# A Mamba-style layer on eight cores: the prefix's convolution and state moved into the main input projection

## The reference, cut to what matters

```python
x = L0_attn_u                                  # [2, 8192, 2048]
xn = _layernorm(x, axis=-1)
# s = recurrent branch
zxbcdt = u @ W_in.T                            # 2048 -> 10304
z, xBC, dt = jnp.split(zxbcdt, [D_INNER, D_INNER + CONV_DIM], axis=-1)
conv = conv_b
for k in range(D_CONV):                        # 4 taps along the sequence
    conv = conv + xp[:, k:k + l, :] * conv_w[:, k]
xBC = jax.nn.silu(conv)
x, B, C = jnp.split(xBC, [D_XB, 2 * D_XB], axis=-1)
dt = jax.nn.softplus(dt + dt_bias);  A = -jnp.exp(A_log)
y = _chunked_scan(xh, dt, A, Bh, Ch, D)        # state carried over the sequence
y = y * jax.nn.silu(z)                         # then a group norm and W_out
g = _silu(_L0_ffn_ref(xn, ...))                # Hadamard transforms, up, gate, down
x = x + s * g
```

## Time and profile before

| what | value |
|---|---|
| median of 2 runs | 10579.05 us (10514.8 and 10643.31) |
| the profiled execution | 10557.54 us |
| its span, slowest core | 10555.9 us |
| spans of the 8 cores | 10456.2 to 10555.9 us |
| granted TensorE clock, mean | 0.755 to 0.761 of full |

### The profile page before, as it was taken

The page is one execution under the profiler, slowest core; times in us unless marked ns, Lnnn a source line. Parts: engine busy times, 40 slices in busy tenths (PEclk is TensorE's granted clock), DMA queues, the critical chain, the costliest instruction groups (busy, mean ns, idle before and its releaser), DMA issues.

```text
span 10555.9 us, 101830 instructions; the slowest of 8 cores (10456.2 to 10555.9 us)
## 1 busy us (share of the span) xinstructions
PE 6530.7 (62%) x30407; PEld 2875.9 (27%) x30407; DVE 3243.3 (31%) x4007; ACT 1924.3 (18%) x2672; POOL 500.0 (5%) x877
## 2 busy tenths in 40 slices
PE   5153361552599994788778777322222399993892
PEld 2021120220344441333333333111111134341341
DVE  3534435335203555111111111354555400002202
ACT  3121121201312332111111111111111211204000
POOL 0000000000000000000000000101001101000000
PEclk9575675775799996898888888655555599795795
DMA  4021120210333220111111111233323344343234
GB/s 101 17 48 43 39 48 19 46 31 3 101 75 70 72 73 18 42 39 40 42 41 37 42 42 40 61 87 94 86 80 87 120 83 104 86 82 130 50 72 165
DMA packets 219991, 675.03 MB, mean 64 GB/s; under 512 B 43230, under 2 KB 101854, under 8 KB 192734
## 3 DMA queue, kind: packets, MB, share of 16 engines
q0 software_dynamic: 74016, 303.36, 15.8%
q1 hardware_dynamic: 145470, 365.16, 10.3%
HBM read 785.31 MB, written 127.67 MB: 86 GB/s over the span
## 4 chain that ended last, share of the span: by engine, by line
PE 55%; DVE 20%; ACT 9%; DMA 7%; issue 6%; DVEq 1%; SPq 1%; ACTq 0%; POOL 0%; POOLq 0%
PE ps L716 11%; PE ps L862 10%; PE ps L1332 9%; PE ps L874 8%; PE ps L496 7%; PE ps L1459 4%; DVE ACCP L524 3%; DVE XWG L600 3%; DMA dcc_scr<-DCC 2%; PE ps L616 2%; ACT X2H L1314 1%; DVE HPB L892 1%; ACT GTT L888 1%; DVE T1B L1030 1%; DVE T1B L1025 1%
## 5 line engine op out<-in xcount | busy, mean ns | idle before, releaser
L716 PE MATMUL ps<-XN,WB 128*128 128x512 bf16 (+1 forms) x6400 | 1178.1, 347 | 15.9 <-DMA WB<-win_blk 15.9
L862 PE MATMUL ps<-XN,WUP 128*128 128x512 bf16 x4096 | 1049.7, 415 | 121.6 <-DMA WUP<-wup_blk 121.6
L874 PE MATMUL ps<-XN,WGT 128*128 128x512 bf16 x4096 | 925.8, 379 | 0.0
L1332 PE MATMUL ps<-X2H,WDB 128*128 128x512 bf16 x4096 | 917.0, 389 | 7.9 <-ACT X2H L1314 7.9
L716 PEld LDWEIGHTS ps<-XN,WB 128*128 128x128 bf16 x6400 | 572.8, 98 | 621.2 <-issue 17.9
L892 DVE SCALAR_TENSOR_TENSOR HPB<-GTT,SUDP,UPT 128x512 bf16<-128x512 bf16 x256 | 192.4, 751 | 1579.5 <-ACT GTT L888 1579.5
L496 PE MATMUL ps<-XNP,WPF 128*128 128x512 bf16 x3072 | 664.4, 379 | 0.3 <-issue 0.3
L862 PEld LDWEIGHTS ps<-XN,WUP 128*128 128x128 bf16 x4096 | 429.6, 105 | 698.6 <-issue 300.9
L1332 PEld LDWEIGHTS ps<-X2H,WDB 128*128 128x128 bf16 x4096 | 408.3, 100 | 516.6 <-issue 108.1
L874 PEld LDWEIGHTS ps<-XN,WGT 128*128 128x128 bf16 x4096 | 400.9, 98 | 483.2
L556 PE MATMUL ps<-DCROW,ONES 1*128 1x64 bf16 x6 | 1.2, 207 | 789.1 <-DMA DCROW<-dcc_scr 789.1
(11 more groups left out here) (194 smaller groups left out, 6808.4 us busy)
## 6 DMA issues: line engine op xcount, KB each, us to landing
CSREP<-csm_scr SPq DMA_DIRECT2D x64, 1024.0 KB
WDB<-wdown_blk POOLq DMA_DIRECT2D x32, 2048.0 KB, 16.4
lnU_p<-u_pfx SPq DMA_DIRECT2D x48, 1024.0 KB
WPF<-win_blk POOLq DMA_DIRECT2D x96, 512.0 KB, 5.2
WB<-win_blk POOLq DMA_DIRECT2D x80, 512.0 KB, 7.0
WUP<-wup_blk POOLq DMA_DIRECT2D x64, 512.0 KB, 5.2
WGT<-wgate_blk POOLq DMA_DIRECT2D x64, 512.0 KB, 7.1
h_scr<-H1T SPq DMA_DIRECT2D x64, 512.0 KB
```

The costliest lines, as they stand in the source:

```text
L716: ins = t.matmul(PS[bank][0:mrows, 0:w], lhs, XN[:, k, o:o + w], start=(k == 0), stop=(k == 15))
L862: ins = t.matmul(PS[bU][:, :], WUP[p][:, k, :], X1[:, k, s4 * 512:(s4 + 1) * 512], start=(k == 0), stop=(k == 15))
L874: ins = t.matmul(PS[bG][:, :], WGT[p][:, k, :], X1[:, k, s4 * 512:(s4 + 1) * 512], start=(k == 0), stop=(k == 15))
L1332: ins = t.matmul(PS[bank][:, :], WDB[p][:, v64, :], X2H[:, v64, s2 * 512:(s2 + 1) * 512], start=(v64 == 0), stop=(v64 == 63))
```

## The change

The prefix pass is split in two. Its first part, phase A, has 12 chunks of 512 positions. It does the layer norm, the projection and the decays, and stores the raw projection to a DRAM scratch `xbcpre_scr`, from two buffers `ZEVP` of 128x512, and the weights of the decay to `wbf_scr`. The weights of the projection are stored as bf16 in `wpfx_scr` during chunk 0; later chunks read them from there, even tiles by SP and odd tiles by POOL. The main layer norm's 17 tiles are spread over the first 6 chunks. The second part, phase B, is a generator `pfxb_gen`: for each of 6 blocks of 1024 it has ten steps: one that loads `XBPRE` back, four with the convolution of 4 tiles each, one with the transposes of the weights `WTQ`, and four with two state groups each. The main input projection calls it once after each of its 81 tiles, so that it is done after m = 59. `SLNEG` becomes one 128x128 tile read with a broadcast; `DIALL` is built at the start of the scan stage instead; `DAM` goes, and its product is formed for each of the 16 chunks there.

```diff
-LCP = 1024
+LCP = 512
 NCHP = PFX // LCP
+LCPB = 1024
+NCHB = PFX // LCPB
...
+            def emit_mms(c):
...
+                        if c == 0:
+                            wW = dma("gpsimd", WPF[wp][:], d_win[32 + mi],
+                                     waits=wpf_free[wp])
+                            wb_tok[mi] = dma("sync", wpfx_scr[mi], WPF[wp][:],
+                                             waits=[wW])
+                        else:
+                            wl = list(wpf_free[wp])
+                            if c == 1:
+                                wl.append(wb_tok[mi])
+                            eng = "sync" if mi % 2 == 0 else "gpsimd"
+                            wW = dma(eng, WPF[wp][:], wpfx_scr[mi], waits=wl)
...
+                        wpf_free[mi % 2] = [tMM]
+                        if c == 0:
+                            wpf_free[mi % 2].append(wb_tok[mi])
...
+                        zevp_free[zp] = dma(
+                            "sync", xbcpre_scr[mi * 128:(mi + 1) * 128,
+                                               c * LCP:(c + 1) * LCP],
+                            ZEVP[zp][:], waits=[aE])
...
+            main_plan = [3, 3, 3, 3, 3, 2, 0, 0, 0, 0, 0, 0]
+            emit_lnc(0)
+            emit_lnc(1)
+            for c in range(NCHP):
+                emit_mms(c)
+                if c % 2 == 1:
+                    emit_dt(c // 2)
+                emit_main_ln(main_plan[c])
+                if c + 2 < NCHP:
+                    emit_lnc(c + 2)
             barrier()
...
+            def pfxb_gen():
...
+                for cb in range(NCHB):
...
+                        ldt.append(dma("sync", dst, src,
+                                       waits=wl0 if mi == 0 else []))
...
+                    yield
...
+                        if mi % 4 == 3:
+                            yield
...
+                        if gb % 2 == 1:
+                            yield
...
+                next(gen, None)
+            for _ in gen:
+                pass
...
+                op("vector", lambda v, slc=slc: v.tensor_scalar(
+                    CTM2[:], DTM[:, slc], AH[:], None, ALU.mult))
```

More of the change, by code:

```diff
@@ L245, in build_program @@
         M1C = sb("M1C", [128, 128], BF16)
[L246 to L247 removed]
+        SLNEG = sb("SLNEG", [128, 128], BF16)
         ONES1 = sb("ONES1", [1, 128], BF16)
@@ L657, in build_program @@
         X1 = XN[:, :, HALO:HALO + TM].rearrange("p a b -> p a b")
-        ln_m = make_ln("m", sba)
-        ln_m(d_u, 0, TL // 128, XN, 0)
-        tD = op("tensor", lambda t: t.matmul(PS[0][:, 0:64], ONES1[:], DROW[:],
-                                             start=True, stop=True),
-                waits=[wG0], inc=True)
-        op("vector", lambda v: v.tensor_copy(DBRD[:], PS[0][:, 0:64]),
-           waits=[tD])
-        op("vector", lambda v: v.tensor_tensor(
-            DIALL[:].rearrange("p (h l) -> p h l", h=64),
-            IDENT[:].unsqueeze(1).broadcast_to([128, 64, 128]),
-            DBRD[:].unsqueeze(2).broadcast_to([128, 64, 128]),
-            ALU.mult))
@@ L743, in build_program @@
                     mi = m - 32
-                    wl = [(S["A"], S["A"].n)]
+                    wl = list(ev_toks)
                     if cvo_free[m % 2] is not None:
                         wl.append(cvo_free[m % 2])
+                    if acc3_prev[0] is not None:
+                        wl.append(acc3_prev[0])
                     op("vector", lambda v, m=m, mi=mi: v.tensor_scalar(
@@ L948, in build_program @@
             DCB6 = sb6("DCB6", [128, 64], F32)
+            DIALL = sb6("DIALL", [128, NH * 128], BF16)
+            DBRD = sb6("DBRD", [128, 64], BF16)
+            tD = op("tensor", lambda t: t.matmul(PS[0][:, 0:64], ONES1[:], DROW[:],
+                                                 start=True, stop=True),
+                    waits=[wG0], inc=True)
+            vDB = op("vector", lambda v: v.tensor_copy(DBRD[:], PS[0][:, 0:64]),
+                     waits=[tD])
+            op("vector", lambda v: v.tensor_tensor(
+                DIALL[:].rearrange("p (h l) -> p h l", h=64),
+                IDENT[:].unsqueeze(1).broadcast_to([128, 64, 128]),
+                DBRD[:].unsqueeze(2).broadcast_to([128, 64, 128]),
+                ALU.mult))
             vZ = op("vector", lambda v: v.memset(Z64[:], 0.0))
```

523 lines of the change are left out of this document (289 added, 234 removed).

## The result

The change made the kernel slower: the ratio to the kernel before is 1.079, with a 95% interval of 1.069 to 1.089. The profiled execution took 11,388.77 us (spans of the cores 11,349.8 to 11,387.2, granted clock 0.747 to 0.748), against 10,557.54. The forecast was 11,250, so the profiled execution took 139 us more.

The account below looks back on a forecast made before the run. TensorE's waits bound the kernel, 1537 us of it wasted in the prefix pass. Phase A 2116, phase B 2558 and 13 make 4687 against 3998: +689 on 10557.5, so 11,250 us, 6% slower; range 10,830 to 11,700.

Parts of the forecast that it names:

- largest term: Phase A's weight loads: each tile serves one strip, SP's load stands behind a store; 77 waits, 454 us, plus clock.
- the loads were not hidden: Rival in phase A: SP's loads land before TensorE runs dry, 593 us less, 10,660 in all; chance 0.09.
- the clock was not at half throughout: Rival in phase A: bursts never get 2.4 GHz, 13.7 us a pair, 385 us more, 11,630; chance 0.13.
- phase B overlapped no better than staged: Rival: phase B overlaps better and weights are hidden, 12 us less in 24 state steps, 10,370; chance 0.04.
- The 77 waits: Phase A, 7 waits for weight loads in each of 11 chunks: 5.9 us each (4.8 to 7.9), 454 us.
- The clock: Phase A: matmuls restart slower after each wait, 1.8 us a gap (0 to 5), 139 us, and 2.5 per chunk start.
- Chunk 0: Phase A's first chunk: f32 load and store to scratch alternate on one buffer, 10 us per two tiles, 90 with clock.
- Layer norms and chains: Phase A: layer norm segments after the chunks 508 us, 12 for seams, and the decay's chains 162 us.
- load step and first convolution step: Phase B, start of a block at m < 32: to the last SiLU 50 us, in a block of 330.
- That interleaving gains little: Phase B: 353 us of matmuls lie under convolutions, 28 main convolutions of 9 us come out, state work stays open.
- The rest: Scan stage: DIALL at its start and 16 small products, some 13 us; SLNEG's broadcast counted at nothing.
- the rival's 10,657: Total if phase A's loads are hidden, given as 10,660; gap and clock under 1.9 us a pair mean under 10,790; chance 0.09.

## Where the prediction was right, and which of its terms failed

**What failed is the size of terms.** The largest are in phase A, the prediction's own "largest term": the wait for a weight load and the clock behind it. I took 4.5 us for the load and 5.9 for the wait; the wait measured 6.4. I took 1.8 us a gap for the clock; with 2.5 at the chunk's start as forecast, 2.2 are left. Over 77 waits that is 72 of the 126 us missing in phase A. Next come the store of chunk 0's copy, and the scan stage's transfers, for which the sum had nothing: 43 us more than forecast, whose cause stays open. The median of all 11 executions, 11,779.37, lies above 11,700, the end of the range: the range had no term for the spread between executions. The two of before that it could rest on gave a median of 10,579.05, ten gave 10,867.79.

**The direction and both mechanisms were right.** The forecast of 11,250 is 1.2% under the profiled execution, which lies in the range. In ratio I said 1.066, just under the interval. The rivals fell: the loads were not hidden (77 waits), the clock was not at half throughout (448 ns a matmul, between 379 and the 634 that it shows at 1.2 GHz), and phase B overlapped no better than staged.

**Phase A: forecast 2116, measured 2242.**
- The 77 waits: 5.9 us forecast, 495.3 / 77 = 6.4 measured, 41 us more. The term mis-sized is the load. I took 4.5 between 3.4 and 6.5; issue to first matmul is 4.88 in the rows above, and the page has 4.6 at the median for SP's loads. The 3.2 us that the prediction estimates from the Trainium skill (DMA: Bandwidth & Descriptors, Anatomy of one DMA) is further off; that section's fit is for transfers that GpSimd issues, and POOL's loads here took 4.1. The measurement decides: with 3.2 us the wait would have been 1.8 us short instead of 0.5.
- The clock: a chunk takes 121.6 us (11 of them 1337.6). Less 58.7 of matmuls and 45.0 of waits, 17.9 are left, where I had 15.1 (7 x 1.8 + 2.5). That is 31 us over 11 chunks. That 1.8 came near is in part luck: the rows left everything from 0 to 5 us a gap open. The rule of the Trainium skill that I weighed (TensorE: Matmul & The Clock Gate, HAM oscillation: waits for transfers between bursts throttle the array each time) is borne out by 7.08 us before and 9.11 behind a gap of 6.2, while behind 1.7 us nothing was lost.
- Chunk 0: 90 forecast, 117 measured, the largest miss in relation. I counted one load (5.2) and one store (4.5) per two tiles. The loads took 6.8 at the median, and eight of POOL's 14 later ones went out only when a store of the copy had landed, in seven of these cases 6.5 to 10 us after its issue. The 11 waits for `win_blk` are 37.5 us, and behind six of them 16 matmuls took 5.1 to 6.4 us instead of 3.6. The longest of these stores was issued at 177.70:

```profile
187.67 0.53 POOL L112 DMA_DIRECT2D WPF<-win_blk  x1 [9.77 <-DMA wpfx_scr<-WPF]
```

- Layer norms and chains: 682 forecast, 706 measured. The segments fit (59 to 62 us for 7 tiles, 41 for 4, against 59 and 40). A chain cost 27 to 31 us, the last 37 with nothing behind it.

**Phase B: forecast 2558, measured 2597.** The three blocks under m = 32 took 342, 341 and 335 us instead of 330; the others 414, 419 and 418 instead of 403, 417 and 417. The term mis-sized is the block's first, load step and first convolution step, 50 us: in the second block it took 62, from the end of the last state matmuls at 2590.0 to the last SiLU at 2652.3, and in the third 59. The later terms fit (82 for three more iterations where I had 83, 6 for 5, 191 for 192). What I did not have is SP's list once more: the 16 loads of `XBPRE` take 12.8 us to issue, the stores of `ZEV` stand behind them, and ScalarE's eviction and the SiLU behind it wait for their buffer. SP and ScalarE:

```profile
2606.94 12.80 SPq L112 DMA_DIRECT2D XBPRE<-xbcpre_scr  x16
2629.39 0.59 ACT L803 CAST ZEV<-ps 128x512 bf16<-128x512 f32 x1 [15.86 <-DMA z_scr<-ZEV]
```

That interleaving gains little was right: undoing it cost 71 us.

**The rest: +13 forecast.** From the first matmul of the up product to the first of the scan 2601 us against 2591 (the 10 us of `DIALL`); the scan stage 1783 against 1736, +47, which I had at 4: slower transfers, shown, but their cause isn't. Behind the scan 67 us less. There the kernel before's core 7, against which I summed, had taken 1356 us from the down product to the output product where its cores 0 to 5 had 1325 to 1328, and 707 to the end (669 on core 0). A forecast should be summed against a core that agrees with the others in each stage.

The sum is 126 + 39 + 44 - 67 = 142, by rounding the 139 us missing. That it is no more is in part luck: the 67 us of the last stages took back a third of what the terms before them had missed. One sum on the way was off, with nothing resting on it: 77 x 1.9 on top of the rival's 10,657 is 10,803, not under 10,790.

## What to carry to other kernels

On an engine or queue that runs its list in order, overlap is decided by what stands ahead, not by what is emitted nearby: put the transfer that a busy engine will need ahead of the stores of results, and split a stage so that each engine's part is issued one step before the next engine needs it. Halving the work per loaded tile turned a hidden load into the bound; two more buffers, or one line in another place, gave it or most of it back. And weave only after asking for each piece which engine stands in order behind it: the same work took 2597, 1912 and 1774 us by its order, with two more buffers in the last two. A load can also stand behind stores whose buffers are late, as the layer norm's did with f32 weights: look at what heads each list at the seam of two stages.

## What the runs showed of the hardware that I had not expected

- The store of 64 decays to `dcc_scr`, 128 bytes as 64 elements from 64 partitions, takes longer than 512 KB of weights, with only the 128 KB store of the decay's weights beside it. In the chain of waits of the change:

```profile
1547.61 17.64 DMA dcc_scr<-DCC
1565.43 0.24 SPq L112
1565.67 0.05 issue
1565.87 5.57 DMA lnU_c<-u_pfx
```

It took 10.0 us on core 0, 14.3 on core 4 and 17.5 on core 1 at the first chain of the same execution; the store is half of a decay's chain.

- Waits of 1.7 us between bursts of 7.07 us left the matmuls at 2.4 GHz; behind waits of 6.2 the same 32 took 9.11 us.
- Large loads (f32 weights, four buffers) were free for their own consumer, but the 128 KB stores beside them took 7.7 us to land instead of 4.4, and each layer norm that followed began 7 to 10 us later.
- Transfers of the scan stage took either of two times on different cores of one execution of the same code, the stage 54 to 70 us apart (1728 to 1732 and 1786 to 1798).
